# Last normalisation joined with the choice of tokens, and the second image's corner table written beside the first group's taps

## The reference

```python
# layer 0
x = x + _L0_conv_ref(_ln_c(x), ...)   # deformable branches, k = 7, 3, 1, 1
t = t + _L0_ffn_ref(_ln_t(t), ...)    # 2 of 8 experts for each token
# layer 1
x = x + _L1_conv_ref(_ln_c(x), ...)   # selective scan
t = _to_tokens(x)
t = t + _L1_ffn_ref(_ln_t(t), ...)    # what follows here

# a branch of _L0_conv_ref
offset = conv2d(x, off_w, off_b, pad)
mask = 2.0 * sigmoid(conv2d(x, mod_w, mod_b, pad))
sampled = bilinear_sample(x, py, px) * mask[:, None]   # 4 corners of each point
y = einsum('bckhw,ock->bohw', sampled, reg_w)

# _L1_ffn_ref: 64 specialists, each takes its 8 best tokens
logits = einsum('bsd,ed->bse', x, gate_w) + gate_b
probs = softmax(logits, axis=1)                # over the tokens of an image
vals, idx = top_k(probs.transpose(0, 2, 1), 8)
pooled = einsum('bked,bke->bed', gathered, topv)
```

## Time and profile before

| | |
|---|---|
| median of 3 runs | 7292.74 us |
| the profiled execution | 7284.9 us, its span 7283.1 us |
| busy: TensorE, VectorE, ScalarE, GpSimd | 5190.9, 5426.3, 4491.8, 4839.4 us |
| first stage | 0 to 115.9 us |
| deformable taps | 115.9 to about 4950 us |
| last normalisation | 6965.6 to 7034 us |
| choice of tokens up to the chosen weights | 7034 to 7079.5 us |

### The profile page before, as it was taken

One profiled execution on the slowest core, in us unless ns is written; L12 is line 12 of the kernel. 1 busy time (PEld: TensorE's weight loads), 2 busy tenths in 40 slices (PEclk: granted clock), 3 DMA queues, 4 the chain that ended last, 5 costly groups with the idle time before them and its releaser, 6 DMA issues. The chain is left out here.

```text
span 7283.1 us, 97166 instructions
## 1 busy us (share of the span) xinstructions
PE 5190.9 (71%) x22750; PEld 3162.6 (43%) x22750; DVE 5426.3 (75%) x10543; ACT 4491.8 (62%) x11843; POOL 4839.4 (66%) x4587
## 2 busy tenths in 40 slices
PE   6766676766766666677676676776889957757758
PEld 6443444444434444344444343333544425626634
DVE  5777777777777777777777777773879989989951
ACT  3666666666666666666666666765346759959820
POOL 2777777777777777777777777771049947918800
PEclk8999999999999999999999999888999978978968
DMA  7787887878878788787887878884100012222235
GB/s 233 240 250 239 248 250 236 251 237 248 250 236 250 239 248 250 236 250 239 248 250 236 250 238 248 302 271 163 31 23 32 31 42 74 103 92 90 101 123 187
DMA packets 588926, 1413.52 MB, mean 194 GB/s; under 512 B 94355, under 2 KB 258464, under 8 KB 583968
## 3 DMA queue, kind: packets, MB, share of 16 engines
q0 software_dynamic: 308224, 1006.95, 45.8%
q1 hardware_dynamic: 278050, 398.16, 16.2%
q10 hardware_dynamic: 2304, 4.20, 0.2%
HBM read 1322.52 MB, written 85.86 MB: 193 GB/s over the span
## 5 line engine op out<-in xcount | busy, mean ns | idle before, releaser
L769 POOL DMA_INDIRECT st_corners<-corner_table,df_rows x3840 | 3642.8, 949 | 1293.0 <-issue 1053.3
L1139 ACT ACTIVATE st_corners<-st_corners,df_share 128x128 f32<-128x128 f32 x3840 | 1225.8, 390 | 1560.5 <-DMA st_corners<-corner_table,df_rows 1534.9
L1042 PE MATMUL df_acc_ps<-df_turned,df_tapw 128*128 128x512 f32 x3840 | 1998.3, 647 | 34.3 <-DMA df_tapw<-in_tap_w_dram 31.0
L1031 PE MATMUL df_turn_ps<-main_ident,df_sampled 128*128 128x128 f32 x3840 | 645.5, 294 | 1439.9 <-DVE df_sampled L815 1386.3
L1031 PEld LDWEIGHTS df_turn_ps<-main_ident,df_sampled 128*128 128x128 f32 x3840 | 443.7, 148 | 2218.9 <-issue 2106.3
L810 DVE TENSOR_TENSOR st_corners<-st_corners,df_part_ps 128x512 f32<-128x512 f32 x960 | 660.0, 687 | 864.0 <-ACT df_part_ps L1139 851.8
L1139 ACT ACTIVATE df_part_ps<-st_corners,df_share 128x128 f32<-128x128 f32 x3840 | 1178.6, 351 | 29.8 <-DVE df_sampled L815 29.4
L324 PE MATMUL st_conv_ps<-st_ow,st_patch 128*128 128x147 f32 (+1 forms) x6272 | 991.3, 305 | 0.0
L1042 PEld LDWEIGHTS df_acc_ps<-df_turned,df_tapw 128*128 128x128 f32 x3840 | 737.9, 210 | 571.6 <-issue 536.6
L324 PEld LDWEIGHTS st_conv_ps<-st_ow,st_patch 128*128 128x128 f32 x6272 | 892.2, 200 | 8.7 <-issue 8.1
L799 DVE TENSOR_TENSOR st_corners<-st_corners,df_weight_ps 128x512 f32<-128x512 f32 x960 | 657.3, 685 | 265.6 <-DMA st_corners<-corner_table,df_rows 262.0
(11 more groups left out here) (370 smaller groups left out, 5679.4 us busy)
## 6 DMA issues: line engine op xcount, KB each, us to landing
df_tapw<-in_tap_w_dram SPq DMA_DIRECT2D x962, 128.0 KB
sc_c_row<-c SPq DMA_DIRECT2D x128, 512.0 KB, 3.7
st_corners<-corner_table,df_rows POOLq DMA_INDIRECT x3840
y_b<-st_outs SPq DMA_DIRECT2D x128, 256.0 KB, 6.3
l1f_w<-in_w_dram SPq DMA_DIRECT2D x32, 1024.0 KB, 6.8
fu_spare<-y_b SPq DMA_DIRECT2D x64, 256.0 KB, 5.4
f_y_in<-y_b SPq DMA_DIRECT2D x64, 256.0 KB, 5.6
u<-dw_u SPq DMA_DIRECT2D x64, 256.0 KB, 2.1
```

Of the source, the lines that this page charges most:

```text
L769: nc.gpsimd.indirect_dma_start(corners[slot][:, j].rearrange("p v c -> p (v c)"), None, tables[g // GPB], bass.IndirectOffsetOnAxis(ap=row ...
L1031: t = nc.tensor.transpose(turn_ps[pair][:, j * TILE:(j + 1) * TILE], sampled[pair][:, j, :], ident[:])
L1042: m = nc.tensor.matmul(acc_ps[:, h, :], tapw[pair][:, h * P:(h + 1) * P], turned_sb[pair][:], start=first, stop=last, skip_group_check=not ...
L1139: nc.scalar.activation(dst, src, ACT.Copy, scale=share[slot][:, j - VT, v:v + 1]).then_inc(weighed_a, 1)
```

## The change

Four edits. (1) The offset weights of the 7x7 branch come by 14 DMAs in place of one, those of columns kx = 0 and 1 first with the bias; TensorE waits for these alone at first, and for the others at the tap (ky, kx) = (0, 2). (2) The 16 DMAs of image 1's table leave the first stage and are issued one by one behind the weight loads of taps 10 to 25 of group 0. The two padded images go to DRAM behind the loads of taps 4 and 6 instead of at the start, and the strip of group 2 is loaded behind tap 8's. (3) The rows of group 1 are shifted straight from `fu.xpad`, with no strip; three copies of an unused accumulator are left out (`done < 0`). (4) `norm_and_choose` replaces `layer_norm` and `choose`: the groups of both images alternate, the code is unrolled, VectorE counts group k + 1 before it normalises group k, three token buffers and eight input buffers are used, the logits of a pair of groups are multiplied as soon as both are transposed back, and the maxima are taken of 512 tokens at a time. The best 8 are sought among the exponentials, while ScalarE scales them.

```diff
-    sp.dma_start(t.ow[:, :, :, 0:C3], d["ow4"]).then_inc(t.loaded, 16)
+    for kx in (slice(0, OW_SPLIT), slice(OW_SPLIT, KMAX)):
+        for ky in range(KMAX):
+            sp.dma_start(t.ow[:, ky, kx, 0:C3], d["ow4"][:, ky, kx, :]).then_inc(t.loaded4[kx.start // OW_SPLIT], 16)
...
+        if c == 0 and half == 0 and (ky, kx) == (0, OW_SPLIT):
+            pe.wait_ge(t.loaded4[1], 16 * KMAX)
+            pe.wait_ge(t.loaded, 16 * OFFSET_LOADS)
...
-            for b in range(B):
-                for part in range(TABLE_PARTS):
-                    sp.wait_ge(normed, b * GPB + (part + 1) * (GPB // TABLE_PARTS))
-                    image(b, part)
+            for part in range(TABLE_PARTS):
+                sp.wait_ge(normed, (part + 1) * (GPB // TABLE_PARTS))
+                for index in range(8):
+                    image(0, part, index)
...
                 for tap in range(LAG, first):
                     load_tap(g, tap, tap % 2)
-                if g == 0:
-                    sp.wait_ge(padded_out, 16 * B)
-                    sp.wait_ge(averaged, 1)
+                    at = tap - LAG - 2
+                    if at in (0, 2):
+                        sp.dma_start(xp_dram[:, at // 2], fu.xpad[:, at // 2]).then_inc(padded_out, 16)
+                    if at == 4:
+                        sp.wait_ge(averaged, 1)
+                        sp.wait_ge(padded_out, 16 * B)
+                        load_strip(nb, ngl)
+                    if 6 <= at < 6 + 8 * TABLE_PARTS:
+                        image(1, (at - 6) // 8, (at - 6) % 8)
...
+                if c == 1:
+                    shift_rows(nc, t, fu.xpad[:, 0, ROWS + row:ROWS + row + HALF_ROWS, :], shifts)
+                    return
```

More of the change, by code:

```diff
@@ L2971, in _, with load @@
         def _(sp):
+            def load(k):
+                b, c = group(k)
+                sp.dma_start(x_in[k % RING][:], x_dram[b, :, c * SPAN:(c + 1) * SPAN]).then_inc(x_loaded[k % RING], 16)
+            for k in range(RING):
+                load(k)
             sp.wait_ge(cleared, 1)
@@ L2976, in _ @@
                 sp.dma_start(gate_b[rows, :], d["gate_b"]).then_inc(loaded, 16)
+            for k in range(RING, GROUPS):
+                sp.wait_ge(tokens, k - RING + 1)
+                load(k)
             for s in range(WSLOTS):
@@ L3035, in _, with count, normalise, top @@
             own = Tally(dve, steps)
-            dve.wait_ge(kept, GPB + 2)
-            own.done(v.tensor_reduce(peak[:], prob[:], AX_X, ALU.max))
+            def count(k):
+                dve.wait_ge(tokens, k + 1)
+                for j in range(TPG):
+                    own.done(v.bn_stats(stats[:, k % 2, j, :], tok_ps[k % BANKS][:, j, :]))
+                own.settle()
+                for j in range(TPG):
+                    own.done(v.bn_aggr(mv[:, k % 2, j, :], stats[:, k % 2, j, :]))
+                own.settle()
+                dve.sem_inc(moments, 1)
+            def normalise(k):
+                b, c = group(k)
+                dve.wait_ge(rooted, k + 1)
+                own.done(v.reciprocal(rstd[:, k % 2, :], std[:, k % 2, :]))
+                own.settle()
+                for j in range(TPG):
+                    own.done(v.tensor_scalar(tok_sb[:, b * TPI + c * TPG + j, :], tok_ps[k % BANKS][:, j, :],
+                                             mv[:, k % 2, j, 0:1], rstd[:, k % 2, j:j + 1], ALU.subtract, ALU.mult))
+                own.settle()
+                dve.sem_inc(normed, 1)
+            def top(c):
+                dve.wait_ge(kept, c + 1)
+                own.done(v.tensor_reduce(peaks[:, c:c + 1], prob[:, c * SPAN:(c + 1) * SPAN], AX_X, ALU.max))
+            v.memset(eps_sb[:], eps).then_inc(constant, 1)
+            count(0)
+            for k in range(GROUPS):
+                if k + 1 < GROUPS:
[5 more added lines that the diff above has]
+                top(c)
+            own.settle()
+            own.done(v.tensor_reduce(peak[:], peaks[:], AX_X, ALU.max))
             own.settle()
```

293 lines of the change are left out of this document (106 added, 187 removed).

## The result

The changed kernel takes **7231.03 us** (median of 4, 7226.04 to 7233.04), the kernel before 7292.35 us (median of 4, 7291.16 to 7294.27): ratio 0.9917, 95% interval 0.9902 to 0.9931. That is 61.3 us less. The profiled execution is the fastest of the four.

A forecast was written before the change was run, and what follows sets the result against it. It took GpSimd's issue of indirect fetches to bound the taps, with three stretches outside that pace. Terms 26.0 + 4.4 - 3 + 7 + 21.9 + 2.4 = 58.7 us off 7292.7 gave 7234 us; likeliest 7224 to 7243, whole range 7220 to 7258.

The forecast's parts named there:

- weights: First stage: offset weights in 14 DMAs let the convolution start near 15 us; 11.9 us gained.
- table out of the first stage: First stage: without image 1's table writes SP's queue no longer ends the stage; 14.1 us gained.
- strip: Start of deformable stage: group 1's rows from `fu.xpad` start the convolution sooner, shortening GpSimd's early wait; 4.4 us gained.
- moved DMAs: Group 0 of deformable stage: padded images and table writes beside the taps cost 3 us, at most 18.
- normalisation: Last normalisation: VectorE's 52.0 us of work plus a slow TensorE start of 3 us; 7 us gained.
- last product to exponential: Last stage: way from VectorE's last product to the exponential takes 5.9 us instead of 27.8; 21.9 us gained.
- exponential to eight best: Choice: the reciprocal and a VectorE instruction leave VectorE's way; 2.4 us gained.
- Rival (c): First stage: weights come no sooner because input loads share the DMAs; 47 us gained in all, 7246; chance 0.1.
- two bounds for the writes: Table writes in group 0: lower 0, all hidden at 407 GB/s; upper 7 us, DMA shares adding.
- Rival (b): Group 0: moved DMAs make GpSimd wait, 18 us lost instead of 3; 44 us gained in all, 7249; chance 0.2.
- Rival (d): Group 0: table writes hold SP, which paces sixteen taps; kernel slower, 7311 at 10 us a tap; chance 0.03.
- Rival (a): Last stage: TensorE stays at 1.2 GHz, normalisation loses 8 us; 42 us gained in all, 7251; chance 0.17.

The follow-up runs named there:

- experiment 2: Changed kernel with the offset weights loaded by one DMA and TensorE waiting for all loads before the convolution's first part: 7249.3 us, ratio 0.9936.
- experiment 1: Changed kernel with image 1's sixteen table writes put back into the first stage: 7255.8 us, ratio 0.9945.
- experiment 4: Changed kernel with group 1's rows read again from the strip loaded at the start of the deformable stage: 7244.5 us, ratio 0.9929.
- experiment 6: Changed kernel with image 1's sixteen table writes issued four to a tap, at taps 10 to 13: 7252.1 us, ratio 0.9946.
- experiment 8: Changed kernel with useless identity transposes filling TensorE (32 at the last stage's start, six ahead of each transposition back), three token banks: 7222.3 us, one execution.
- experiment 3: Kernel before with only the last normalisation and choice replaced by `norm_and_choose`: 7264.3 us, ratio 0.9954.
- experiment 9: Changed kernel with four token banks, early padded images, last transposition before logits 6: 8958.0 us (slow chip), 7220.6 elsewhere; slow-chip runs also unaltered, 8987.9, and two writes per tap, 8973.8.

## Why the prediction was right

The prediction was 7234 us, with 7224 to 7243 as its likeliest case; 7231 was measured. Its steps against the profile, in us gained:

| step | predicted | measured | from |
|---|---|---|---|
| weights | 11.9 | 11.0 | experiment 2 |
| table out of the first stage | 14.1 | 14.6 | experiment 2 |
| strip | 4.4 | 5.6 | 48.0 to 42.3 us into the stage |
| moved DMAs | -3 | -1.8 | one wait of 2.06, less the usual 0.30 |
| normalisation | 7 | 5.0 | 62.15 to 57.2 |
| last product to exponential | 21.9 | 20.4 | 27.8 to 7.4 |
| exponential to eight best | 2.4 | 2.5 | 6.4 to 3.9 |
| sum | 58.7 | 57.3 | |

The span fell by 58.8. The rest, 1.5, is what is left of larger things that the sum doesn't have: fetches at 1.2521 in place of 1.2534 us, +4.8 by the last of them; the stages from it to the last normalisation, -2.5 (from the last fetch to the first moments 2024.4 us before, 2026.9 after, and 2023.2 to 2030.2 in the other traces at the usual pace, with no relation to the edits); -0.9 behind the choice. That the sum agrees within 2 us is thus partly luck. That each step does is in part luck too: the groups of the same last stage took 57.1 to 59.8 us in seven traces, so "5.0" is 2.3 to 5.1, and the profiled execution is near the good end of it. The first stage's two terms, the tail and the search are beyond such scatter.

*First stage.* Part 0 came at 15.95 (said: 15), the stage ended at 90.34 (said: 89.9), ScalarE last. Rival (c) is out. The step's hidden condition is experiment 1's: taken singly, the weights bring 7.2 us where the table is still there, and the table 14.6 where the weights are still late; the rest needs both.

*Strip.* The convolution started 3.2 us into the stage, as said. The prediction named one cause, the copy; experiment 4 finds two of about equal weight.

*Moved DMAs.* The size was nearly right and the cause not: the prediction weighed sixteen table writes and two padded images alike, and only the images cost anything (2.06 us here, up to 3.6 in two waits in the trace of four banks). Of its two bounds for the writes, 0 held at one to a tap. The rule behind the upper one, that shares add, was not shown anywhere: at one to a tap the engines were full too (share 1.00 to 1.07) and nothing was lost, and at four the weights' place behind the writes was the pace. The Trainium skill (DMA: Bandwidth & Descriptors, Queues, rings and completion order) says that an engine works off each ring in order; the trace agrees, in that TensorE waited 3 us for weights that stand behind a padded image in SP's queue:

```profile
156.31 3.64 PE L900 MATMUL df_acc_ps<-df_turned,df_tapw 128*128 128x512 f32 x4 [3.05 <-DMA df_tapw<-in_tap_w_dram]
...
169.21 0.69 DVE L657 TENSOR_TENSOR st_corners<-st_corners,df_weight_ps 128x512 f32<-128x512 f32 x1 [3.10 <-DMA st_corners<-corner_table,df_rows]
```

The prediction had this stall at 5.7 us, twice; it came once (3.05 at tap 5, 0.39 at tap 7). The second row shows the other half: with the images beside them the fetched corners came late, and VectorE waited for them, 5.79 us at 156 and 3.10 at 169, ahead of GpSimd's 2.06. Rival (b) had the place right, but 1.8 us and not 18. Rival (d), with SP as the pace, fails at 0.59 us a write, one to a tap; at four to a tap its mechanism is what experiment 6 shows, and even that took back only 21 of the 61 us.

*Normalisation.* The forecast was 52.0 us of VectorE's own work and a slow start of 3 us, for which no row stood, with the full clock afterwards: 55 us. Measured were 57.2: 53.3 of VectorE's own work, as the executions with four banks show, and 3.8 of waits. So of the 2 us that the step fell short by, 1.3 are VectorE's work, put too low at 3.1 us a group, and 0.8 the waits. The start was slow indeed (0.50 until about 6952), but the clock came and went. Rival (a), half clock throughout, was wrong as stated, right as to the place: all four of VectorE's waits stand behind logits that began at the lower clock. The Trainium skill (TensorE: Matmul & The Clock Gate, Part 1: The HAM clock gate) calls the throttled state the default; the trace agrees, and experiment 8 shows that work without a use is enough to leave it.

*Tail.* 7.4 us, where 5.3 to 7.6 was the range and 5.9 the choice: logits 6 ran for the most part at the lower clock (2.93 us) and the last transposition back stood behind them. The clock is the cause that the runs bear out: with logits 6 at 1.00 the tail was 6.55 us with fillers and 5.90 in experiment 3, while moving the transposition ahead gained nothing (experiment 9).

*Range.* Its lower end, 7220 for "up to 72 us gained", does not follow from the terms: with nothing lost, no slow start and the shortest tail they add up to 26.0 + 4.4 + 10 + 22.5 + 2.4 = 65.3 us, 7227. The measured time doesn't hang on it.

## What to carry to other kernels

Two gains ahead of one barrier are not separate: with the table writes in place, 4 of the weights' 11 us would have been lost, so find what would end the stage once the first is gone. Work moved under a long loop can be free at one density and dear at another: one 512 KB write to a tap cost nothing, four cost 21 us, because a small load that the loop needs stood behind them in the same queue. Ask not only whether the engines have room, but what stands behind the moved work. Where an engine waits for TensorE at its lower clock, one more buffer did as much as a clock kept up by work without a use.

## What the runs showed of the hardware

The pace of GpSimd's fetches differs between executions. Fetches from 400 us on, with count, duration (least/median/most, ns) and first and last start, in the changed kernel and in experiment 2:

```profile
L627 POOL DMA_INDIRECT st_corners<-corner_table,df_rows x3604: 942/946/1345, 399.9 to 4911.1; - x190
```

```profile
L621 POOL DMA_INDIRECT st_corners<-corner_table,df_rows x3615: 945/949/1377, 400.0 to 4938.2; - x191
```

That is (4911.1 - 399.9)/3603 = 1.2521 us a fetch and 1.2557, 13 us over the stage, on the same instructions; the least was 1.2516 (experiment 6). Of eleven traces from chips at their usual pace three had the median of 949 ns, all three from one chip in the same series of runs, where a fourth kernel had 946. What sets it stays open; this kernel, bound by GpSimd's issue, can't be compared by single times to better than 0.2%.

The 24% of experiment 9 lie in the long loops: stalls of mostly 8 to 9 us about every four taps of the deformable stage, and none in the unrolled first stage and last normalisation, which kept their lengths. From 400 to 2000 us the DMA share was 0.59 at 174 GB/s in the changed kernel, where it is 0.80 at 246 GB/s at the usual pace. The profile names no resource for it: ScalarE's waits there are put down to a remote semaphore. It stays open.
